# Attention beside a mixture of experts: weighted sums of two attention units in one group, the maxima unit behind the transposition one pair of heads later, and two sets of loads into stacks that are done

## The chip, the cores and the metric

The kernel runs on one core of a Trainium2 chip. The time is that of the device for one launch, in microseconds (us); smaller is better. The engines are TensorE (PE; its weight loads are PEld), VectorE (DVE), ScalarE (ACT), GpSimd (POOL) and SyncE (SP), which issues most of the DMAs. They run side by side and wait for one another by semaphores.

## The reference

The input x has 4 batches of 1024 rows of 256 numbers, in float32. Its rows are normalised (layernorm, xn). The output is x + attention(xn) + experts(xn).

```python
q, k, v = xn @ Wq, xn @ Wk, xn @ Wv                  # 16 heads of 16
scores = where(j <= i, q @ k.T, -1e30) + slope[h] * (j - i)
w = softmax(scores / sqrt(16))
attention = (w @ v) @ Wo + bo
...
# each row goes to the 2 best of 8 experts by router logits
expert(x) = (gelu(x @ Wgate) * (x @ Wup)) @ Wdown * per_expert_scale
experts = sum over the 2 of weight * expert(xn)
```

## The kernel before

The kernel has five stages, one behind the other: `project` (layernorm, the projections, router logits), `route` (the experts' choice), `attend` (attention, and the map of rows to experts on the side), `experts` (72 tiles of 128 rows), `combine`. The change lies in `attend`, and in where the loads of the experts' gate and up weights (`w_gu`) and of the x rows for `combine` go.

`attend` goes through 16 steps t, one for each batch and quad of four heads. The queries and keys of a quad lie as stacks of bf16 parts (`qs`, `ks`, four buffers each, loaded three steps ahead by `load_quad` from SP, L150), so that a single matmul gives scores with float32-like accuracy, with the slope's term and the row's negated maximum as further rows of the stack.

A step has two kinds of work on TensorE.

The first is the scores and sums of this quad. The causal 1024x1024 triangle of a head is cut into 9 attention units of 512 columns (`UNITS`, L55). For each unit and head TensorE makes the scores (`scores`, L831, into the ring `spsum` of three), ScalarE takes their exp into `probs` (`exp`, L778; a unit has one of `PRING` = 3 slots), POOL zeroes the diagonal tiles (`mask_unit`, L715), and TensorE adds the weighted sums of the values for the four heads into `cpsum` (`weighted`, L839). These are float32 matmuls of 17 columns of weights, the four heads in four column tiles of the array (`tile_position`). `weighted` is issued in halves; 8 matmul instructions are 256 columns of all four heads. ScalarE copies `cpsum` to `ctxT` twice a step: the low rows behind the exp of unit 3, head 2 (L798), the high rows behind the first exp of the next step's unit 1 (L802).

The second is the row maxima for a quad one or two steps ahead. They come in maxima units (`ITEMS`, L98; `item` L813 on TensorE, L733 on VectorE): 18 of 1024 columns each into one of two slots of `mpsum` (`RING` = 2), which VectorE reduces (L742), and a nineteenth, number NI - 1 = 18, that transposes the finished maxima (L829); VectorE splits the result into three bf16 parts (L749 to L755), and SP writes it to the stack as further rows (`maxima_rows`, L666). The first score of the next step waits for them.

The order on TensorE is written out by hand. A step has 18 pairs of heads p (`PAIRS`), two for each unit: pairs 0 and 1 score unit 1, 2 and 3 unit 2, and so on, and pairs 16 and 17 score unit 0 of the next step. In a pair come a score, the pair's maxima units (`PAIR_ITEMS`, L107), the other score, and then the weighted sums that `PV_AT` (L92) gives it:

```python
for h in (2 * (p % 2), 2 * (p % 2) + 1):
    scores(n, hq1, u, h)
    if h % 2 == 0:
        for ahead, k in PAIR_ITEMS[p]: item(...)
for u0, half in PV_AT[p]: weighted(t, b, hq, u0, half)
```

Before the change `PV_AT` has groups in pairs 1, 3, 4, 7, 9, 11, 13, 15 and 17: unit 0; unit 1; the low half of unit 2; the high half of unit 2 with unit 3; units 4, 5, 6, 7 and 8. `PAIR_ITEMS` has one maxima unit in each pair: numbers 8 to 17 of the next quad in pairs 0 to 9, and 0 to 7 of the quad after it in pairs 10 to 17, with the transposition ahead of number 1 in pair 11. A maxima unit's matmuls wait until VectorE has taken the one two before. The first exp of a unit waits (L783) until the sums of the unit that had its slot are done.

SP issues, in `attend`, first the lists for POOL's map and the first row of maxima, then the eight loads of `w_gu` (L680), then in each step `load_quad` for three steps ahead, the next quad's row of maxima (L668) and the lists for the map. POOL issues four indirect DMAs per step for the map, behind the masks of unit 2 (L712).

Of the kernel before, what the change touches and what calls it, by code (L numbers as in the profile page):

```python
# [18 lines left out]
P = 128  # L19
F32 = mybir.dt.float32  # L20
# [13 lines left out]
DH = D // P  # L34
# [49 lines left out]


PV = [pv_pieces(u) for u in range(NU)]
PRING = 3
SRING = 3


PAIRS = 2 * NU
PV_AT = [[] for _ in range(PAIRS)]  # L92
for _u in range(NU):
    PV_AT[2 * _u + 1] = [(_u, 0), (_u, 1)]
PV_AT[4], PV_AT[5], PV_AT[7] = [LOW_LAST], [], [HIGH_FIRST, (3, 0), (3, 1)]


ITEMS = []  # L98
# [8 lines left out]
def pair_items():  # L107

    first = NI - 1 - LEAD
    out = [[(1, LEAD + p)] for p in range(first)] + [[(2, k)] for k in range(LEAD)]
    out[first + 1].insert(0, (1, NI - 1))
    return out


# [13 lines left out]
ITEM_NO = item_orders()  # L130


def head_buffers(nc, ctx):

    sb = lambda name, shape, dt=F32: ctx.enter_context(nc.sbuf_tensor(name, shape, dt))
    sem = lambda name: ctx.enter_context(nc.semaphore(name))
    return {
        "qs": [sb(f"qs{i}", [ROWS, 4, S], BF16) for i in range(NQ)],
        "ks": [sb(f"ks{i}", [ROWS, 4, S], BF16) for i in range(NQ)],
        "vs": [sb(f"vs{i}", [P, KT, 4, VW]) for i in range(NQ)],  # L140
        "stack_in": [sem(f"stack_in{i}") for i in range(NQ)],
        "v_in": [sem(f"v_in{i}") for i in range(NQ)],
        "const_in": sem("const_in"),
    }
# [464 lines left out]
def attend(nc, ins, scratch, keep, heads):  # L609
# [3 lines left out]
    with ExitStack() as ctx:  # L613
# [50 lines left out]
        @block.sync  # L664
        def _(sp):
            def maxima_rows(n, hq):  # L666
                sp.wait_ge(max_split, n + 1)
                sp.dma_start(qs[hq][R_MAX:ROWS, :, :], mparts[:, hq % 2, :]).then_inc(mrow_in[hq], 16)  # L668

            def tile_entries(t, par):  # L670

                sp.dma_start(entries[:, par], keep["entries"][:, :, ds(2 * t, 2), :]).then_inc(entries_in[par], 16)
                sp.dma_start(slots[:, par], keep["slot"][:, :, ds(2 * t, 2)]).then_inc(entries_in[par], 16)

            for t in range(2):
                tile_entries(t, t)
            maxima_rows(0, 0)

            for e in range(NE):
                sp.dma_start(keep["w_gu"][:, e * DH:(e + 1) * DH], ins["w_gu"][:, e * DH:(e + 1) * DH]).then_inc(keep["w_gu_in"], 16)  # L680

            def body(t, b, hq, has):
                par = hq % 2
                if has(3):
                    sp.wait_ge(pv_done, PRING + NU * t)
                    load_quad(sp, scratch, heads, *quad(b, hq, 3))
                if has(1):
                    maxima_rows(t + 1, (hq + 1) % NQ)
                sp.wait_ge(entries_out[par], 64 * (2 * b + hq // 2 + 1))
                if has(2):  # L690
                    tile_entries(t + 2, par)

            steps(sp, body)
            for i in range(2):
                sp.wait_ge(entries_out[i], 64 * (B * NQ // 2))

        @block.gpsimd
        def _(pool):
            def body(t, b, hq, has):
                for j in range(1, NU + 1):  # L700
                    if j == NU and not has(1):
                        continue
                    mask_unit(NU * t + j, j % NU)
                    if j == LOW_LAST[0]:
                        map_entries(b, hq)

            def map_entries(b, hq):
                par = hq % 2
                wait_apart(pool, entries_in[par], 32 * (2 * b + hq // 2 + 1))
                for i in range(2):  # L710
                    for k in range(2):
                        pool.indirect_dma_start(scratch["map"], bass.IndirectOffsetOnAxis(ap=slots[:, par, k, i:i + 1].bitcast(U32), axis=0),  # L712
                                                entries[:, par, k, i, :], None).then_inc(entries_out[par], 16)

            def mask_unit(n, u):  # L715

                if not DIAG[u]:
                    return
                wait_apart(pool, exp_done, 4 * n + 4 + SRING)
                for c in DIAG[u]:  # L720
                    part = probs[:, u % PRING, :, c:c + P]
                    pool.affine_select(out=part, in_=part, compare_op=ALU.is_ge, fill=0.0, base=0,  # L722
                                       pattern=[[0, 4], [1, P]], channel_multiplier=-1).then_inc(masked, 1)

            mask_unit(0, 0)
            steps(pool, body)
# [47 lines left out]
        @block.scalar  # L774
        def _(act):
            act.sem_inc(exp_done, SRING)

            def exp(n, u, h):  # L778

                m = 4 * n + h  # L780
                act.wait_ge(s_ready, m + 1)
                if h == 0:
                    act.wait_ge(pv_done, n + 1)  # L783
                act.activation(probs[:, u % PRING, h], spsum[:, (4 * u + h) % SRING], ACT.Exp, scale=SCALE).then_inc(exp_done, 1)  # L784

            for h in range(4):
                exp(0, 0, h)
            exp(1, 1, 0)

            def body(t, b, hq, has):  # L790
                for j in range(1, NU + 1):
                    u, n = j % NU, NU * t + j
                    if j < NU or has(1):
                        for h in range(1 if j == 1 else 0, 4):
                            exp(n, u, h)
                            if (j, h) == (3, 2):
                                act.wait_ge(low_done, t + 1)
                                act.activation(keep["ctxT"][:, ds(t, 1), 0:CH].rearrange("p a c -> p (a c)"), cpsum[:, :], ACT.Copy).then_inc(ctx_taken, 1)  # L798
                if has(1):
                    exp(NU * t + NU + 1, 1, 0)  # L800
                act.wait_ge(pv_done, NU * t + NU + PRING)
                act.activation(keep["ctxT"][:, ds(t, 1), CH:S].rearrange("p a c -> p (a c)"), cpsum[:, :], ACT.Copy).then_inc(ctx_taken, 1)  # L802

            steps(act, body)

        @block.tensor
        def _(pe):
# [31 lines left out]
            def weighted(t, b, hq, u, half):  # L839
# [12 lines left out]
                    pe.wait_ge(masked, MASKED[NU] * t + MASKED[u] + needs)  # L852
                for i, (c, kt, q0, w) in enumerate(pieces):
                    for h in range(4):
                        last = pe.matmul(cpsum[32 * h:32 * h + VW, q0 % CH:q0 % CH + w], vs[hq][:, kt, h], probs[:, u % PRING, h, c:c + w],  # L855
                                         start=i == 0 and (u, half) in ((0, 0), HIGH_FIRST),
                                         stop=(u, half) == LOW_LAST or kt == KT - 1, tile_position=(0, 32 * h), skip_group_check=True)
                if (u, half) == LOW_LAST:
# [16 lines left out]
            def body(t, b, hq, has):  # L875
                for p in range(PAIRS):
                    j = p // 2 + 1
                    u, n = j % NU, NU * t + j
                    b1, hq1 = quad(b, hq, 1) if j == NU else (b, hq)
                    for h in (2 * (p % 2), 2 * (p % 2) + 1):  # L880
                        if j < NU or has(1):
                            if u == 0 and h == 0:
                                pe.wait_ge(mrow_in[hq1], 16 * (b1 + 1))
                            scores(n, hq1, u, h)
                        if h % 2 == 0:
                            for ahead, k in PAIR_ITEMS[p]:
                                if has(ahead):
                                    item(t + ahead, *quad(b, hq, ahead), k)
                    for u0, half in PV_AT[p]:
                        weighted(t, b, hq, u0, half)  # L890

# [363 lines left out]
def build(nc, ins, out):  # L1255
    with ExitStack() as ctx:
# [8 lines left out]
            "slot": sb("slot", [P, 2, NT], I32),  # L1265
            "entries": sb("entries", [P, 2, NT, 2], I32),
            "tile_expert": sb("tile_expert", [1, NST], I32),
            "w_gu": sb("w_gu", [P, NE * DH, 2 * HID]),
            "w_gu_in": ctx.enter_context(nc.semaphore("w_gu_in")),
            "ctxT": sb("ctxT", [P, B * NQ, S]),  # L1270
        }
# [4 lines left out]
            "map": nc.dram_tensor("slot_map", [NST * P, 2], I32).ap(),  # L1276
            "y": nc.dram_tensor("expert_rows", [2 * TOK + NST * P, D], F32).ap(),
        }
        project(nc, ins, scratch, keep)
        with ExitStack() as held:  # L1280
            heads = head_buffers(nc, held)
            route(nc, ins, scratch, keep, heads)
            attend(nc, ins, scratch, keep, heads)
        last_weights = {"w_o": sb("w_o", [P, DH, D]), "bias": sb("bias", [P, D]), "x": sb("x_rows", [P, NT, D]),
                        "in": ctx.enter_context(nc.semaphore("wo_in")), "x_in": ctx.enter_context(nc.semaphore("x_rows_in"))}
        experts(nc, ins, scratch, keep, last_weights)
        combine(nc, ins, scratch, keep, last_weights, out)
# [61 lines left out]
```

## Time and profile before

| | us |
|---|---|
| median of 3 runs | 939.3 |
| lowest, highest | 938.69, 1016.51 |
| the profiled execution | 941.12 |
| its span, first to last instruction | 939.4 |
| mean granted TensorE clock | 0.937 |

| engine | busy us | share |
|---|---|---|
| TensorE matmul | 812.5 | 86% |
| TensorE weight load | 426.3 | 45% |
| VectorE | 562.1 | 60% |
| ScalarE | 483.2 | 51% |
| GpSimd | 390.0 | 42% |

The attention's TensorE work goes from 159.1 to 627.5 us. In a timeline each row is a start in us from the span's start, a length in us, the engine, the line of the kernel, the operation, out<-in with shapes, and how many instructions of that kind the row merges; in brackets stands how long the engine had been idle before it and what ended the wait. TensorE's ends are modelled, so lengths overlap the next start; the time of a piece is the difference of two starts.

### The profile page before, as it was taken

To read this page: it belongs to the slowest core of one execution; us is meant where nothing else is said; L and a number is where in the kernel's file an instruction comes from. 1 tells how busy PE (TensorE), PEld (TensorE's weight loads), DVE (VectorE), ACT (ScalarE), POOL (GpSimd) and SP (SyncE) were. 2 spreads that over 40 slices of the span, in tenths; PEclk is the share of its full clock that TensorE was granted. 3 is DMA by queue.
4 is the path that set the end of the run, shared out by engine and by line. 5 is a ranking of instruction groups with operands and counts; after the bars stand their busy time and mean duration, and the time that the engine had idled before them with its cause. 6 is when DMAs were issued, how large, how long until landed. Compare 5 with 4: busy or idle time off the path is not lost. (4 is left out here: it accounts for less than half of the span.)

```text
span 939.4 us, 17505 instructions
## 1 busy us (share of the span) xinstructions
PE 812.5 (86%) x5618; PEld 426.3 (45%) x5619; DVE 562.1 (60%) x1560; ACT 483.2 (51%) x1011; POOL 390.0 (42%) x456
## 2 busy tenths in 40 slices
PE   5989601799999999999999999856999999999598
PEld 2555400134444444444444444313555656555497
DVE  4767364988888888888888888301222222222177
ACT  2333300067777777777777777852333333333374
POOL 3545340033223233322323332323666666665398
PEclk9999855589999999999999999996999999999799
DMA  4999899295555666555566600009222222222485
GB/s 157 221 263 269 213 107 121 34 253 74 62 61 57 82 81 81 67 62 61 59 82 81 81 3 3 2 6 321 86 84 84 84 84 84 84 85 78 129 245 182
DMA packets 115004, 100.32 MB, mean 107 GB/s; under 512 B 58172, under 2 KB 95676, under 8 KB 114876
## 3 DMA queue, kind: packets, MB, share of 16 engines
q1 hardware_dynamic: 105976, 80.50, 46.9%
q0 software_dynamic: 8960, 18.95, 6.4%
q8 instruction: 37, 0.61, 0.3%
q14 instruction: 31, 0.25, 0.1%
HBM read 63.89 MB, written 35.00 MB: 105 GB/s over the span
## 5 line engine op out<-in xcount | busy, mean ns | idle before, releaser
L784 ACT ACTIVATE probs<-spsum 128x512 f32<-128x512 f32 x576 | 312.1, 604 | 169.6 <-PE spsum L835 163.8
L742 DVE CUSTOM_DVE_ANT_0 junk<-mpsum,mask 128x128 bf16<-128x128 f32 (+7 forms) x512 | 360.0, 754 | 58.5 <-issue 51.7
L824 PE MATMUL mpsum<-ks,qs 102*128 102x512 bf16 (+3 forms) x768 | 183.5, 343 | 45.9 <-DVE cpsum L731 26.3
L722 POOL TENSOR_SCALAR_AFFINE_SELECT probs<-probs 128x512 f32<-128x512 f32 x128 | 78.8, 634 | 340.8 <-ACT probs L784 340.8
L835 PE MATMUL spsum<-qs,ks 105*128 105x512 bf16 (+3 forms) x768 | 199.2, 329 | 10.6 <-ACT probs L784 8.3
L855 PE MATMUL cpsum<-probs,vs 128*17 128x256 f32 (+2 forms) x2560 | 152.7, 360 | 1.5 <-POOL probs L722 0.8
L1037 PE MATMUL gu<-w_gu,xTs 128*128 x288 | 139.2, 607 | 1.7 <-ACT xTs L981 1.7
L1016 DVE COPY hT<-hp 128x256 f32<-128x256 f32 x72 | 30.6, 425 | 167.8 <-PE hp L1044 100.6
L824 PEld LDWEIGHTS mpsum<-ks,qs 102*128 102x128 bf16 x768 | 69.8, 100 | 122.5 <-DVE maxima L742 39.8
L835 PEld LDWEIGHTS spsum<-qs,ks 105*128 105x128 bf16 x768 | 67.1, 97 | 102.9 <-ACT probs L784 52.9
L956 POOL DMA_INDIRECT expert_rows<-y,places x72 | 70.7, 983 | 72.2 <-ACT y L990 42.2
L855 PEld LDWEIGHTS cpsum<-probs,vs 128*17 128x17 f32 x2560 | 59.8, 97 | 77.4 <-issue 36.4
L951 POOL DMA_INDIRECT rows<-xn_rows,places x72 | 69.3, 962 | 34.9 <-issue 20.7
L985 ACT ACTIVATE gate<-gu 128x256 f32<-128x256 f32 x72 | 27.7, 384 | 100.7 <-issue 64.0
L1050 PE MATMUL yp<-w_down,hT 128*128 x288 | 74.2, 380 | 0.4 <-issue 0.4
L1037 PEld LDWEIGHTS gu<-w_gu,xTs 128*128 128x128 f32 x288 | 52.1, 193 | 45.4 <-issue 38.5
L712 POOL DMA_INDIRECT slot_map<-entries_now,slots x64 | 61.8, 966 | 17.2 <-issue 17.2
L417 PE MATMUL qkpsum<-xT,w_qk 128*128 128x512 f32 x128 | 59.8, 612 | 4.4 <-DVE rest L359 3.3
L1014 DVE TENSOR_TENSOR hid<-gu,gate 128x256 f32<-128x256 f32 x72 | 30.2, 420 | 49.3 <-ACT gate L985 49.3
L1050 PEld LDWEIGHTS yp<-w_down,hT 128*128 128x128 f32 x288 | 49.1, 190 | 4.6 <-issue 0.9
L312 POOL TENSOR_TENSOR parts<-rest,parts 128x512 bf16<-128x512 f32 x32 | 37.0, 1157 | 32.0 <-DVE parts L361 32.0
L990 ACT ACTIVATE y<-yp 128x256 f32<-128x256 f32 x72 | 27.7, 384 | 36.2 <-issue 31.8
(124 smaller groups left out, 698.5 us busy)
## 6 DMA issues: line engine op xcount, KB each, us to landing
qk_parts<-parts SPq DMA_DIRECT2D x32, 384.0 KB, 4.4
qs<-qk_parts SPq DMA_DIRECT2D x96, 128.0 KB
ks<-qk_parts SPq DMA_DIRECT2D x96, 128.0 KB
yk<-expert_rows SPq DMA_DIRECT2D x32, 256.0 KB, 3.1
v_rows<-vt SPq DMA_DIRECT2D x32, 136.0 KB, 4.5
vs<-v_rows SPq DMA_DIRECT2D x16, 272.0 KB, 12.0
x_in<-in_x SPq DMA_DIRECT2D x8, 512.0 KB, 6.3
xn_rows<-xn SPq DMA_DIRECT2D x8, 512.0 KB, 5.8
```

The costliest lines, as they stand in the source:

```text
L417: last = pe.matmul(qkpsum[:, q % 2], w_qk[:, dh, q], xT[:, par, dh], start=dh == 0, stop=dh == DH - 1)
L712: pool.indirect_dma_start(scratch["map"], bass.IndirectOffsetOnAxis(ap=slots[:, par, k, i:i + 1].bitcast(U32), axis=0), entries[:, par, k, ...
L722: pool.affine_select(out=part, in_=part, compare_op=ALU.is_ge, fill=0.0, base=0, pattern=[[0, 4], [1, P]], channel_multiplier=-1).then_inc ...
L742: last = dve.tensor_tensor_reduce(junk[:, slot, c:c + w], mpsum[:, slot, c:c + w], keep["mask"][:, S - w:S], 1.0, 3 * NEG, ALU.add, ALU.ma ...
L784: act.activation(probs[:, u % PRING, h], spsum[:, (4 * u + h) % SRING], ACT.Exp, scale=SCALE).then_inc(exp_done, 1)
L824: last = pe.matmul(mpsum[:, slot, at + c:at + e], qs[hq][0:R_MAX, h, qt * P:(qt + 1) * P], ks[hq][0:R_MAX, h, c:e], start=True, stop=True)
L835: last = pe.matmul(spsum[:, (4 * u + h) % SRING, c:c + w], ks[hq][:, h, kt * P:(kt + 1) * P], qs[hq][:, h, q0:q0 + w], start=True, stop=True)
L855: last = pe.matmul(cpsum[32 * h:32 * h + VW, q0 % CH:q0 % CH + w], vs[hq][:, kt, h], probs[:, u % PRING, h, c:c + w], start=i == 0 and (u, ...
L951: pool.indirect_dma_start(rows[:, s % RR], None, scratch["xn"], bass.IndirectOffsetOnAxis(ap=places[:, s, 0:1].bitcast(U32), axis=0)).then ...
L956: pool.indirect_dma_start(scratch["y"], bass.IndirectOffsetOnAxis(ap=places[:, s, 1:2].bitcast(U32), axis=0), y[:, s % RR], None).then_inc ...
L1037: last = pe.matmul(gu[:, par], xT[:, par, dh], w_gu[:, ds(e * DH + dh, 1)].rearrange("p a c -> p (a c)"), start=dh == 0, stop=dh == DH - 1)
L1050: last = pe.matmul(yp[:, par, 0:D], hT[:, par, dh], w_down[:, ds(e * DH + dh, 1)].rearrange("p a c -> p (a c)"), start=dh == 0, stop=dh == ...
```

## The change

- `PRING` goes from 3 to 4, and the slot of a unit in `probs` is its running number n modulo 4 (n = 9 t + u).
- The groups of weighted sums are in pairs 1 (unit 0), 4 (unit 1 and the low half of unit 2), 7 (the high half of unit 2 and unit 3), 11 (units 4 and 5), 15 (6 and 7) and 17 (8).
- The transposition stays in pair 11, alone; maxima unit 1, which stood behind it, goes to pair 12. Where a pair has two units, the second now follows the second score.
- The stacks `qs` and `ks` are one tensor, and `w_gu` (first half of it) and the x rows (second half) are views of the same bytes. The eight loads of `w_gu` go out in steps 13 and 14, four each, when the quads that lay there are done; the x rows are loaded where they were, at the start of `experts`.

```diff
-PRING = 3
+PRING = 4
...
 PAIRS = 2 * NU
 PV_AT = [[] for _ in range(PAIRS)]
-for _u in range(NU):
-    PV_AT[2 * _u + 1] = [(_u, 0), (_u, 1)]
-PV_AT[4], PV_AT[5], PV_AT[7] = [LOW_LAST], [], [HIGH_FIRST, (3, 0), (3, 1)]
+PV_AT[1] = [(0, 0), (0, 1)]
+PV_AT[4] = [(1, 0), (1, 1), LOW_LAST]
+PV_AT[7] = [HIGH_FIRST, (3, 0), (3, 1)]
+PV_AT[11] = [(4, 0), (4, 1), (5, 0), (5, 1)]
+PV_AT[15] = [(6, 0), (6, 1), (7, 0), (7, 1)]
+PV_AT[17] = [(8, 0), (8, 1)]
...
-    out[first + 1].insert(0, (1, NI - 1))
+    out[first + 1], out[first + 2] = [(1, NI - 1)], out[first + 1] + out[first + 2]
...
-def head_buffers(nc, ctx):
+def head_buffers(nc, ctx, stacks):
...
-        "qs": [sb(f"qs{i}", [ROWS, 4, S], BF16) for i in range(NQ)],
-        "ks": [sb(f"ks{i}", [ROWS, 4, S], BF16) for i in range(NQ)],
+        "qs": [stacks[0:ROWS, i, 0] for i in range(NQ)],
+        "ks": [stacks[0:ROWS, i, 1] for i in range(NQ)],
...
-            for e in range(NE):
-                sp.dma_start(keep["w_gu"][:, e * DH:(e + 1) * DH], ins["w_gu"][:, e * DH:(e + 1) * DH]).then_inc(keep["w_gu_in"], 16)
-
             def body(t, b, hq, has):
                 par = hq % 2
                 if has(3):
                     sp.wait_ge(pv_done, PRING + NU * t)
                     load_quad(sp, scratch, heads, *quad(b, hq, 3))
+                elif has(1):
+                    sp.wait_ge(pv_done, PRING + NU * t)
+                    for e in range(NE // 2 * (t % NQ - 1), NE // 2 * (t % NQ)):
+                        sp.dma_start(keep["w_gu"][:, e * DH:(e + 1) * DH], ins["w_gu"][:, e * DH:(e + 1) * DH]).then_inc(keep["w_gu_in"], 16)
...
-                    part = probs[:, u % PRING, :, c:c + P]
+                    part = probs[:, n % PRING, :, c:c + P]
...
-                        if h % 2 == 0:
-                            for ahead, k in PAIR_ITEMS[p]:
-                                if has(ahead):
-                                    item(t + ahead, *quad(b, hq, ahead), k)
+                        for ahead, k in PAIR_ITEMS[p][h % 2:h % 2 + 1]:
+                            if has(ahead):
+                                item(t + ahead, *quad(b, hq, ahead), k)
...
-            "w_gu": sb("w_gu", [P, NE * DH, 2 * HID]),
+            "stacks": sb("stacks", [P, NQ, 2, 4, S], BF16),
...
+        words = lambda a: a.rearrange("p i s h t -> p (i s h t)").bitcast(F32)
+        keep["w_gu"] = words(keep["stacks"][:, 0:2]).rearrange("p (e h) -> p e h", h=2 * HID)
...
-        last_weights = {"w_o": sb("w_o", [P, DH, D]), "bias": sb("bias", [P, D]), "x": sb("x_rows", [P, NT, D]),
+        last_weights = {"w_o": sb("w_o", [P, DH, D]), "bias": sb("bias", [P, D]), "x": words(keep["stacks"][:, 2:4]).rearrange("p (t d) -> p t d", d=D),
```

## Rows read from the trace of the kernel before

**Rows 1.** The page, 40 slices of the span: TensorE's busy share in tenths.
```profile
PE   5989601799999999999999999856999999999598
```

**Rows 2.** Windows: one step, busy us and instructions; then clock, DMA share, GB/s.
```profile
402.54:430.06 27.52, 26.17 (x258) 11.77 (x257) 23.54 (x69) 20.32 (x39) 8.78 (x12) 1.00 0.58 70
```

**Rows 3.** TensorE's timeline, one step and the last step's transposition.
```profile
400.45 1.06 PE L855 MATMUL cpsum<-probs,vs 128*17 128x256 f32 x16
401.44 0.39 PE L835 MATMUL spsum<-qs,ks 105*128 105x512 bf16 x1
401.67 0.60 PE L824 MATMUL mpsum<-ks,qs 102*128 102x512 bf16 x2
402.11 0.59 PE L835 MATMUL spsum<-qs,ks 105*128 105x512 bf16 x2
402.54 0.27 PE L829 MATMUL mpsum<-ident,maxima 128*32 128x128 f32 x1
403.73 0.61 PE L824 MATMUL mpsum<-ks,qs 102*128 102x512 bf16 x3 [0.92 <-DVE maxima L742]
404.18 0.38 PE L835 MATMUL spsum<-qs,ks 105*128 105x512 bf16 x1
404.49 1.06 PE L855 MATMUL cpsum<-probs,vs 128*17 128x256 f32 x16
...
422.75 0.92 PE L835 MATMUL spsum<-qs,ks 105*128 105x512 bf16 x2
...
424.26 1.49 PE L855 MATMUL cpsum<-probs,vs 128*17 128x256 f32 x24
425.68 0.39 PE L835 MATMUL spsum<-qs,ks 105*128 105x512 bf16 x1
...
426.78 0.59 PE L824 MATMUL mpsum<-ks,qs 102*128 102x512 bf16 x2
427.66 0.39 PE L835 MATMUL spsum<-qs,ks 105*128 105x512 bf16 x1 [0.28 <-ACT probs L784]
...
429.19 0.60 PE L824 MATMUL mpsum<-ks,qs 102*128 102x512 bf16 x2
...
595.00 0.27 PE L829 MATMUL mpsum<-ident,maxima 128*32 128x128 f32 x1
595.17 0.39 PE L835 MATMUL spsum<-qs,ks 105*128 105x512 bf16 x1
```

**Rows 4.** VectorE's timeline, in the same step.
```profile
415.00 0.69 DVE L742 CUSTOM_DVE_ANT_0 junk<-mpsum,mask 128x512 bf16<-128x512 f32 x1 [0.31 <-issue]
...
423.36 1.09 DVE L742 CUSTOM_DVE_ANT_0 junk<-mpsum,mask 128x896 bf16<-128x896 f32 x1
...
424.59 0.95 DVE L742 CUSTOM_DVE_ANT_0 junk<-mpsum,mask 128x768 bf16<-128x768 f32 x1
...
427.20 0.82 DVE L742 CUSTOM_DVE_ANT_0 junk<-mpsum,mask 128x640 bf16<-128x640 f32 x1 [1.30 <-issue]
...
429.97 1.23 DVE L742 CUSTOM_DVE_ANT_0 junk<-mpsum,mask 128x1024 bf16<-128x1024 f32 x1 [0.24 <-issue]
...
431.12 0.27 DVE L749 TENSOR_SCALAR mparts<-mpsum 32x128 bf16<-32x128 f32 x1
...
432.60 1.09 DVE L742 CUSTOM_DVE_ANT_0 junk<-mpsum,mask 128x896 bf16<-128x896 f32 x1 [0.33 <-DVE mparts L755]
```

**Rows 5.** ScalarE's timeline, in the same step.
```profile
422.13 0.59 ACT L798 ACTIVATE ctxT<-cpsum 128x512 f32<-128x512 f32 x1
...
427.01 2.07 ACT L784 ACTIVATE probs<-spsum 128x512 f32<-128x512 f32 x4 [1.83 <-PE spsum L835]
```

**Rows 6.** SP's timeline: the weights' loads, and a row of maxima.
```profile
186.71 4.14 SPq L680 DMA_DIRECT2D w_gu<-in_w_gu  x8
...
432.36 0.79 SPq L668 DMA_DIRECT2D qs<-mparts  x1
```

**Rows 7.** POOL's timeline: the fourth indirect DMA of the step.
```profile
424.84 0.96 POOL L712 DMA_INDIRECT slot_map<-entries_now,slots  x1 [0.30 <-issue]
```

More of the change, by code:

```diff
@@ L783, in exp @@
                     act.wait_ge(pv_done, n + 1)
-                act.activation(probs[:, u % PRING, h], spsum[:, (4 * u + h) % SRING], ACT.Exp, scale=SCALE).then_inc(exp_done, 1)
+                act.activation(probs[:, n % PRING, h], spsum[:, (4 * u + h) % SRING], ACT.Exp, scale=SCALE).then_inc(exp_done, 1)
             for h in range(4):
@@ L854, in weighted @@
                     for h in range(4):
-                        last = pe.matmul(cpsum[32 * h:32 * h + VW, q0 % CH:q0 % CH + w], vs[hq][:, kt, h], probs[:, u % PRING, h, c:c + w],
+                        last = pe.matmul(cpsum[32 * h:32 * h + VW, q0 % CH:q0 % CH + w], vs[hq][:, kt, h], probs[:, n % PRING, h, c:c + w],
                                          start=i == 0 and (u, half) in ((0, 0), HIGH_FIRST),
@@ L1278, in build @@
         }
+        words = lambda a: a.rearrange("p i s h t -> p (i s h t)").bitcast(F32)
+        keep["w_gu"] = words(keep["stacks"][:, 0:2]).rearrange("p (e h) -> p e h", h=2 * HID)
         project(nc, ins, scratch, keep)
         with ExitStack() as held:
-            heads = head_buffers(nc, held)
+            heads = head_buffers(nc, held, keep["stacks"])
             route(nc, ins, scratch, keep, heads)
             attend(nc, ins, scratch, keep, heads)
-        last_weights = {"w_o": sb("w_o", [P, DH, D]), "bias": sb("bias", [P, D]), "x": sb("x_rows", [P, NT, D]),
+        last_weights = {"w_o": sb("w_o", [P, DH, D]), "bias": sb("bias", [P, D]), "x": words(keep["stacks"][:, 2:4]).rearrange("p (t d) -> p t d", d=D),
                         "in": ctx.enter_context(nc.semaphore("wo_in")), "x_in": ctx.enter_context(nc.semaphore("x_rows_in"))}
```

## The prediction

> **What bounds the kernel now.** I read the page's slices first: TensorE is busy for nine tenths or more of each slice of the attention, a little less where it begins and ends [rows 1]. The change touches attention and two sets of loads, so everything is decided there. The windows view of one step (one batch's quad of four heads, transposition to transposition) gives 27.52 us: TensorE 26.17 busy at a granted clock of 1.00, the upper level throughout, VectorE 23.54, ScalarE 20.32 [rows 2]. No engine is far from the limit, so I turned to TensorE's own order of time, where the starts matter, not the busy time, because its ends are modelled.
>
> There the pieces are (starts subtracted, [rows 3]):
> - A maxima unit of 1024 columns is 2 matmuls: 401.67 to 402.11, 0.44 us. A score matmul of 512 columns is 0.22 (two of them from 402.11 to 402.54). A pair of heads, with two scores and a unit, is 0.87.
> - A group of 16 weighted-sum matmuls (one attention unit) lasts from 400.45 to 401.44, 0.99; one of 24 at this width from 424.26 to 425.68, 1.42. Eight more cost 0.43, so 16 are 0.86 of work, and 0.13 goes when TensorE leaves the column tiles. Entering costs too: the score at 404.18 is followed by the group 0.31 later, where a score is otherwise 0.22. A group in and out costs 0.22.
> - The transposition at 402.54 is followed by a maxima unit only at 403.73: 1.19, of which the row puts 0.92 down to VectorE. In the last step no maxima unit stands behind it and it takes 0.17 (595.00 to 595.17). The stall is 1.02.
> - From 426.78 to 427.66 a maxima unit takes 0.88, not 0.44: 0.44 of wait for ScalarE. Two scores at 422.75 last 0.92, where two last 0.59 at 402.11: 0.33 more.
> The stalls of a step are 1.02 + 0.44 + 0.33 = 1.79; what is left, 25.73, is issue.
>
> VectorE is the other half. A maxima unit of two tiles takes 1.23 from start to start (423.36 to 424.59), one of a single 1024-column tile 1.15 (429.97 to 431.12) [rows 4]. A step has 14 of the former and 4 of the latter, 21.8, and the transposition's four instructions with what follows, 431.12 to 432.60, 1.48: 23.3 us. The other 4.2 are gaps of 0.2 to 0.4 after a single group and one of 1.30 after the long group at 424.26 [rows 4]. They come from the ring of two mpsum slots: while TensorE is in a group, VectorE has at most two units left, 2.4 us less what it had done of them.
>
> **The change, part by part.**
> *Fewer groups.* Nine groups per step become six (pairs 1, 4, 7, 11, 15, 17): 3 x 0.22 = 0.66 us less issue, 10.6 us over 16 steps. The matmuls are the same.
> The TensorEngine Tiling (Array Packing) page of the Trainium skill (Key Properties) says that a change of tiling mode drains the array, and its page TensorE: Matmul & The Clock Gate (Step-by-step: what each phase is for) puts a drain at some 128 cycles. By that an estimate for entry and exit at the upper clock would be 0.11 us, half of what the rows show, and 5 us in place of 10.6; I go by the rows.
>
> *Unit behind the transposition later.* The transposition stays in pair 11; the unit behind it follows the first score of pair 12. Between them come a score (0.22), a double group (4 x 0.43 + 0.22 = 1.94) and a score: 2.4 us, more than the stall. The 1.02 goes. But pair 12 now has two units.
>
> *Four probability slots.* The exp of unit 5 must wait today for the first sum of the group at 424.26; after that wait ScalarE resumes at 427.01, although its score began at 425.68 and 0.43 is the usual distance, and this gives TensorE's 0.44 [rows 3, 5]. With four slots it waits for unit 1, summed in pair 4, long before. No other unit's slot is late either: unit 6 needs unit 2 (pair 7), 7 needs 3 (pair 7), 8 needs 4 (pair 11), and so on. The 0.44 goes. The 0.33 stays: a copy of the sums sits in ScalarE's order at 422.13 [rows 5].
>
> *What is late next.* Bunching leaves stretches in which TensorE makes a maxima unit every 0.87 us and VectorE takes one every 1.22, with two slots between. Set TensorE's leaving of a group at 0. Score to 0.22, unit to 0.66, its last matmul at 0.44; VectorE, idle by then, begins 0.55 behind that, at 1.0 (the unit at 429.19 has its second matmul 0.22 later, at 429.41, and VectorE, which had idled for 0.24, starts on it at 429.97: 0.55 [rows 3, 4]) and is through at 2.3 (1.23 and the 0.08 of the last read), so the third unit behind a group can't start before 2.35, the fourth before 3.6, then one per 1.23.
> - Pairs 12 to 15 hold 8 scores and 5 units, 3.95 of issue. The fifth starts at 4.8, and with it and a score the stretch ends at 5.5: 1.55 of stall (before, with groups in pairs 13 and 15: none).
> - Pairs 2 to 4: the third unit could start at 1.96: 0.40.
> - Pairs 5 to 7: the same wait, most of it within the 0.33 of ScalarE: 0.35 in all.
> - Pairs 8 to 11: 0.40 for the unit of pair 10, and 0.35 for the transposition, which waits for the unit of pair 9.
> Sum 3.05 against 1.79 before: +1.26. VectorE tells the same: its gaps become about 0.9 + 1.4 + 0.3 + 0.5 + 0.8 + 0.8 = 4.7 (a gap grows by what a group grows, 0.86 to 0.93 over the 0.3 to 0.5 of a single one), and 23.3 + 4.7 = 28.0.
> This is worked from starts and not shown by any row, so bounds: no new stall at all (-0.66 - 1.02 - 0.44 = -2.1 us a step), if VectorE's gap behind a double group were the 0.3 of a single one; and +2.6, if after every long group the signals come late as at 427.01 (below).
>
> *Gate and up weights.* Eight loads are issued from 186.71 on, ahead of a quad's loads [rows 6]. They now go out four and four in steps 13 and 14, where SP has no quad to load. Behind them on SP is the row of maxima, which goes out 2.3 us after the transposition (432.36 against 430.06), two thirds of a step, some 17 us, behind the loads; eight of these took 4.14 us to issue, so four are long out of the way. The experts use them only after the attention. Cost 0, with the 17 us as cover; without it a row of maxima would come late by up to the 4.14 that eight take to issue, in steps 13 and 14: 0 to 8 us. The x rows go to another address at the same moment: 0.
>
> *Sum.* A full step: -0.66 + 1.26 = +0.6. Fourteen of them 8.4; step 14 lacks the units for two steps ahead, step 15 has none and ScalarE sets its pace: +0.7 together. +9 us. The profiled execution took 941.1 (span 939.4), so 950.2; the runs shown have 939.3 as median, 1.8 below it: 948. Chances below go by 2%, 19 us, which is about what a measurement of this kernel can tell from no change.
>
> **Rivals.**
> *Signals late after each long group (slower).* Behind the group of 24 (1.42 us) ScalarE begins 1.33 after the score's start instead of 0.43, and VectorE at 427.20, 0.5 late as well [rows 3 to 5]. If the length of the group does that, and not unit 5's wait nor POOL's fourth indirect DMA at 424.84, which ends beside it [rows 7], the change has four such groups (1.42, 1.42, 1.94, 1.94). Each puts 0.5 into VectorE's round, which now sets the pace, and 0.9 in front of ScalarE, so between 0.5 and 0.9, say 0.67, for each of three more: +2.0 a step on top of 0.6. 16 x 2.6 = 41: 980. It turns to slower by over 2% from two more late groups on (+1.3 a step): 962. Against it: unit 5's wait explains ScalarE's part, and behind the group of 16 at 400.45 nothing is late.
> *VectorE keeps up (faster).* Issue and stalls removed, nothing new: -2.1 x 15 = -32, 907. It needs VectorE's gaps at 25.4 - 23.3 = 2.1 over six groups, 0.35 each; rows show that behind single groups, but 1.30 behind the long one. Half of it gives 923.
> *Everything cancels.* The stalls of pairs 12 to 15 come out a third smaller, and the time stays at 939 to 941. The same mechanism with other sizes; it lies in the forecast's range.
>
> **How the numbers follow.** Forecast with its sizes (935 to 960): 0.63. Late signals: 0.22, of which 0.19 beyond 958. VectorE keeps up, wholly or half: 0.15, of which 0.10 beyond -19 us. The range 924 to 972 leaves out the full late signals (about 0.11) and the full gain (0.08). Likeliest 948, its own range 935 to 960. Faster 0.10, same 0.70, slower 0.20.
>
> **What would show it.** Right: steps of 27.9 to 28.3; groups of 32 matmuls 1.85 long; no 0.92 behind the transposition; new waits of TensorE for VectorE in pairs 12 to 15, three of them, adding to about 1.5; the exp of unit 5 no more than 0.45 behind its score. Wrong: a step below 27, with VectorE's gap behind the double groups under 0.6 (then VectorE isn't what sets the pace), or gaps of 1.3 to 1.9 behind every long group (the late signals). TensorE's waits for a row of maxima in steps 14 and 15 would show the weights' loads in the way.

## The result, and the profile after

The kernel after the change takes 959.8 us as median against 940.4 of the kernel before beside it: a ratio of 1.020, with an interval of 1.016 to 1.023. One of the four runs of the kernel before, of 1016.5 us, fell in a slower state of the chip and is left out of the ratio; the median of its other three is 939.3. So it is slower, by 19 to 20 us, where 9 were forecast; whether that is over 2% the interval leaves open. The profiled execution was its quickest run, 955.5 us, with a span of 953.8 against 939.4.

The 14.4 us between the spans come from two places. From the first maxima matmul to the last weighted sum the attention takes 485.7 us against 468.2, +17.4. The experts take 236.0 against 238.7, -2.7, and that is no part of the change: two of the experiments below, `ring4` and `later`, have the same code there and take 238.6 and 235.9. What differs is the granted clock of the first 10 us of that stage, 0.50 before and 0.77 after.

The attention is read from one step, as in [rows 2]. First the page's slices of the kernel after, to be set beside [rows 1]:

```profile
PE   5999502799999999999999999983999999999598
```

The windows view of the ninth step after (columns as in [rows 2]):

```profile
409.60:438.22 28.62, 26.29 (x258) 11.97 (x258) 23.28 (x69) 20.26 (x39) 8.81 (x12) 1.00 0.57 67
```

The step is 1.1 us longer than in [rows 2] at the same clock, with the same count of instructions and VectorE's and ScalarE's busy time hardly changed. The busy columns say nothing of the cause; the starts do. TensorE's timeline of the same step after:

```profile
409.61 0.27 PE L833 MATMUL mpsum<-ident,maxima 128*32 128x128 f32 x1 [0.20 <-DVE maxima L746]
409.71 0.38 PE L839 MATMUL spsum<-stacks 105*128 105x512 bf16 x1
410.02 1.92 PE L859 MATMUL cpsum<-probs,vs 128*17 128x256 f32 x32
411.88 0.39 PE L839 MATMUL spsum<-stacks 105*128 105x512 bf16 x1
...
413.19 0.38 PE L839 MATMUL spsum<-stacks 105*128 105x512 bf16 x1
414.25 0.61 PE L828 MATMUL mpsum<-stacks 102*128 102x512 bf16 x3 [0.67 <-DVE maxima L746]
...
415.47 0.61 PE L828 MATMUL mpsum<-stacks 102*128 102x512 bf16 x2 [0.18 <-DVE maxima L746]
...
416.69 0.61 PE L828 MATMUL mpsum<-stacks 102*128 102x512 bf16 x3 [0.18 <-DVE maxima L746]
...
427.35 0.61 PE L828 MATMUL mpsum<-stacks 102*128 102x512 bf16 x3 [0.23 <-DVE maxima L746]
...
429.54 0.39 PE L839 MATMUL spsum<-stacks 105*128 105x512 bf16 x1
...
431.17 0.39 PE L839 MATMUL spsum<-stacks 105*128 105x512 bf16 x1
432.14 0.39 PE L839 MATMUL spsum<-stacks 105*128 105x512 bf16 x1 [0.58 <-ACT probs L788]
...
434.54 0.39 PE L839 MATMUL spsum<-stacks 105*128 105x512 bf16 x1
...
437.00 0.59 PE L828 MATMUL mpsum<-stacks 102*128 102x512 bf16 x2 [0.28 <-DVE maxima L746]
...
438.22 0.27 PE L833 MATMUL mpsum<-ident,maxima 128*32 128x128 f32 x1 [0.20 <-DVE maxima L746]
```

Read it against [rows 3]. The transposition is followed by a score after 0.10, so the 1.02 behind it is gone. The groups of 32 last 1.86 (410.02 to 411.88), as forecast. The prices are again differences of starts less 0.22 for a matmul of 512 columns (the row's own figure in brackets is smaller, since it goes by modelled ends):

| stretch | stalls in the row order | sum | forecast |
|---|---|---|---|
| pairs 12 to 15 | 0.83, 0.34, 0.34 | 1.51 | 1.55 |
| pairs 2 to 4 | 0.39 | 0.39 | 0.40 |
| pairs 5 to 7 | 0.10, 0.76 | 0.86 | 0.35 |
| pairs 8 to 11 | 0.45, 0.36 | 0.81 | 0.75 |
| all | | 3.57 | 3.05 |

What is left, 28.62 - 3.57 = 25.05, is issue, 0.64 less than the 27.52 - 1.83 = 25.69 of the step before: 0.21 for each of three groups saved, as the rows had it (0.22). The 1.83 is taken from starts too: 0.44, 0.31 for the copy, and 1.08 behind the transposition, which takes 0.11 where nothing holds it (409.61 to 409.71); the prediction's 1.02 had 0.17 for it, from the last step. The estimate from the Trainium skill's page TensorE: Matmul & The Clock Gate (Step-by-step: what each phase is for), 0.11 for a way in and out, is not what this kernel shows.

So one line is off, pairs 5 to 7. There stands ScalarE, whose timeline after (the first of the two) answers to [rows 5], and beside it POOL's (the second), which answers to [rows 7]:

```profile
430.51 0.60 ACT L788 ACTIVATE probs<-spsum 128x512 f32<-128x512 f32 x1 [1.70 <-PE spsum L839]
...
435.18 4.23 ACT L788 ACTIVATE probs<-spsum 128x512 f32<-128x512 f32 x8 [1.10 <-PE spsum L839]
```

```profile
429.19 0.98 POOL L716 DMA_INDIRECT slot_map<-entries_now,slots  x1 [0.16 <-issue]
430.47 0.96 POOL L716 DMA_INDIRECT slot_map<-entries_now,slots  x1 [0.31 <-issue]
431.74 0.96 POOL L716 DMA_INDIRECT slot_map<-entries_now,slots  x1 [0.30 <-issue]
433.00 0.96 POOL L716 DMA_INDIRECT slot_map<-entries_now,slots  x1 [0.30 <-issue]
```

The exp begins 0.97 behind the start of its score (429.54 to 430.51), where 0.43 is usual, and that of unit 5 0.64 behind (434.54 to 435.18), although its slot is long free. They begin 1.32 and 5.99 behind the start of POOL's first indirect DMA at 429.19. The second distance is the one of the kernel before. POOL's first of the four there:

```profile
421.04 0.98 POOL L712 DMA_INDIRECT slot_map<-entries_now,slots  x1 [0.16 <-issue]
```

The exp of unit 5 at 427.01 [rows 5] stands 5.97 behind 421.04, and in all full steps of both kernels the distance of unit 5's exp lies between 5.92 and 6.05. That is a mark of POOL's DMAs, not of a slot that comes free. The experiments test it.

### The profile page after: what moved, and what is told of

The parts are those of the page before. It is cut to its first block and busy times, and to the rows that moved or that the text cites. A ratio compares the mean times of both kernels' runs of the same rounds, so it can differ in the third digit from the quotient of the medians.

```text
span 953.8 us, 17505 instructions
## 1 busy us (share of the span) xinstructions
PE 817.6 (86%) x5618; PEld 429.6 (45%) x5619; DVE 558.2 (59%) x1560; ACT 482.2 (51%) x1011; POOL 390.9 (41%) x456
## 5 line engine op out<-in xcount | busy, mean ns | idle before, releaser
L746 DVE CUSTOM_DVE_ANT_0 junk<-mpsum,mask 128x128 bf16<-128x128 f32 (+7 forms) x512 | 356.4, 754 | 77.1 <-issue 59.2
L828 PE MATMUL mpsum<-stacks 102*128 102x512 bf16 (+3 forms) x768 | 184.0, 344 | 53.5 <-DVE cpsum L735 26.4
L839 PE MATMUL spsum<-stacks 105*128 105x512 bf16 (+3 forms) x768 | 197.6, 330 | 11.1 <-ACT probs L788 7.1
L859 PE MATMUL cpsum<-probs,vs 128*17 128x256 f32 (+2 forms) x2560 | 145.0, 363 | 0.4 <-ACT ctxT L806 0.2
L1040 PE MATMUL gu<-stacks,xTs 128*128 x288 | 137.3, 599 | 1.8 <-ACT xTs L984 1.8
L828 PEld LDWEIGHTS mpsum<-stacks 102*128 102x128 bf16 x768 | 67.1, 100 | 140.2 <-DVE maxima L746 54.1
L839 PEld LDWEIGHTS spsum<-stacks 105*128 105x128 bf16 x768 | 68.4, 97 | 97.4 <-ACT probs L788 34.5
L859 PEld LDWEIGHTS cpsum<-probs,vs 128*17 128x17 f32 x2560 | 64.8, 98 | 71.4 <-issue 29.7
L1040 PEld LDWEIGHTS gu<-stacks,xTs 128*128 128x128 f32 x288 | 51.6, 191 | 44.5 <-issue 37.6
```

Source lines behind the costliest of these rows:

```text
L746: last = dve.tensor_tensor_reduce(junk[:, slot, c:c + w], mpsum[:, slot, c:c + w], keep["mask"][:, S - w:S], 1.0, 3 * NEG, ALU.add, ALU.ma ...
L828: last = pe.matmul(mpsum[:, slot, at + c:at + e], qs[hq][0:R_MAX, h, qt * P:(qt + 1) * P], ks[hq][0:R_MAX, h, c:e], start=True, stop=True)
L839: last = pe.matmul(spsum[:, (4 * u + h) % SRING, c:c + w], ks[hq][:, h, kt * P:(kt + 1) * P], qs[hq][:, h, q0:q0 + w], start=True, stop=True)
L1040: last = pe.matmul(gu[:, par], xT[:, par, dh], w_gu[:, ds(e * DH + dh, 1)].rearrange("p a c -> p (a c)"), start=dh == 0, stop=dh == DH - 1)
```

## The experiments

Changes are described against the kernel after, save `before_spread`, which changes the kernel before. "Step" is the mean distance of two transpositions over 14 steps, "last step" what lies between the last transposition and the last weighted sum.

| kernel | ratio to before | step us | last step us |
|---|---|---|---|
| before | 1 | 27.49 | 32.22 |
| after | 1.020 (1.016 to 1.023) | 28.53 | 35.11 |
| ring4 | 0.9996 (0.998 to 1.001) | 27.39 | 32.11 |
| later | 0.9975 (0.996 to 0.999) | 27.27 | 32.09 |
| groups | 1.022 (1.020 to 1.024) | 28.77 | 34.91 |
| map8 | 1.059 (1.056 to 1.063) | 30.63 | 33.85 |
| after_mapend | 1 run | 28.08 | 32.27 |
| later_mapend | 1 run | 26.93 | 31.11 |
| after_half | 1 run | 26.67 | 34.88 |
| before_spread | 0.9939 (0.992 to 0.996) | 27.05 | 31.60 |
| after_spread | 1.012 (1.010 to 1.015) | 28.37 | 32.50 |
| later_spread | 0.9939 (0.992 to 0.996) | 26.93 | 31.59 |
| placed | 0.987 (0.984 to 0.989) | 26.58 | 31.27 |

**One part at a time: ring4, later, groups.** `ring4` puts back the groups and the places of the maxima units, and so keeps the fourth slot and the loads into the stacks:

```diff
-PV_AT[1] = [(0, 0), (0, 1)]
...
-PV_AT[17] = [(8, 0), (8, 1)]
+for _u in range(NU):
+    PV_AT[2 * _u + 1] = [(_u, 0), (_u, 1)]
+PV_AT[4], PV_AT[5], PV_AT[7] = [LOW_LAST], [], [HIGH_FIRST, (3, 0), (3, 1)]
...
-    out[first + 1], out[first + 2] = [(1, NI - 1)], out[first + 1] + out[first + 2]
+    out[first + 1].insert(0, (1, NI - 1))
```

`later` puts back the groups alone, `groups` the places alone.

> The changed kernel with the old groups of weighted sums and the old place of the maxima unit behind the transposition; what is left of the change is the fourth probability slot and the two sets of loads. Theory 1 (the slot: ScalarE resumes late at unit 5 because it waits for the slot): the exp of unit 5 begins 0.43 us behind its score, a step falls from 27.5 to 27.1 us, the time by some 6 us to 934. Theory 2 (POOL's four indirect DMAs hold up the waking of engines that wait): the exp of unit 5 still begins 5.9 to 6.0 us after the first of the step's four indirect DMAs, a step stays at 27.4 to 27.5 and the time at 939 to 941. The loads cost nothing by either.

> As ring4 but with the maxima unit behind the transposition in pair 12, as in the change; old groups. The 1.08 us stall behind the transposition goes from pair 11; by the ring of two mpsum slots most of it comes back as one wait of about 0.9 in pairs 12 and 13, so a step is 0.2 us shorter than in ring4: 27.3, the time 3 us under ring4's. The rival (the stall was a pure loss that cover removes) gives 1.0 less: 26.5 and 15 us under ring4's.

> As ring4 but with the new six groups of weighted sums; the unit behind the transposition stays in pair 11. If the groups are what costs, with three of them 0.66 us less issue and the waits for VectorE in pairs 12 to 15, 8 to 11 and 2 to 4 more, a step is 0.2 above the changed kernel's 28.55: 28.7 to 28.9, the time 962 to 965. If it is the combination of both edits that costs (two units in pair 12), a step is at or below 27.5 and the time at or below 941.

`ring4`: 937.6 us against 937.8. The slots and the loads together are worth nothing measurable. With four slots the exp of unit 5 still begins 1.21 behind its score (422.79 to 424.00), which is 5.86 behind POOL's first indirect DMA, and TensorE still waits 0.33 for it. ScalarE's timeline, then POOL's:

```profile
424.00 2.06 ACT L785 ACTIVATE probs<-spsum 128x512 f32<-128x512 f32 x4 [1.72 <-PE spsum L836]
```

```profile
418.14 0.98 POOL L713 DMA_INDIRECT slot_map<-entries_now,slots  x1 [0.16 <-issue]
```

`later`: 936.0 us. The 1.02 behind the transposition goes, but the step is only 0.12 shorter than in `ring4`. TensorE's timeline shows the wait again, one pair later, for the same VectorE:

```profile
400.82 0.27 PE L830 MATMUL mpsum<-ident,maxima 128*32 128x128 f32 x1
400.93 0.38 PE L836 MATMUL spsum<-stacks 105*128 105x512 bf16 x1
...
403.55 0.38 PE L836 MATMUL spsum<-stacks 105*128 105x512 bf16 x1
404.72 0.61 PE L825 MATMUL mpsum<-stacks 102*128 102x512 bf16 x3 [0.80 <-DVE maxima L743]
```

`groups`: 958.8 us, +21, all of the loss and a little more. So the six groups carry it. Its mean step of 28.77 holds one of 30.20, in which TensorE's clock fell for 3.4 us; without that one it is 28.66, so moving the unit takes 0.13 a step off with the new groups, as it takes 0.12 off with the old ones. The windows row of the fall:

```profile
354.72:358.13 3.41, 3.41 (x31) 1.25 (x33) 1.83 (x7) 0.60 (x1) 0.00 (x0) 0.50 0.08 8
```

**POOL's indirect DMAs elsewhere: map8.** The four are issued behind the masks of unit 8, near the end of the step's row of units, where the groups around them have 24 and 16 matmuls.

```diff
-                    if j == LOW_LAST[0]:
+                    if j == 8:
                         map_entries(b, hq)
```

> The changed kernel with POOL's four indirect DMAs of a step issued behind the masks of unit 8 (pair 15 on) instead of unit 2 (pair 4 on). Theory 2 (they hold up waking engines): the waits of pairs 5 to 8 beyond the ring's own (some 0.4 to 0.5 us a step) go, and late wakings now stand within 6 us of the new place, where TensorE waits for no one: step 28.0 to 28.15, the time 6 to 8 us under the changed kernel's. Theory 1 or a cause in the long groups themselves: the late wakings stay behind the groups of pairs 4 and 7 and a step stays at 28.5.

It takes 992.7 us, 5.9% more than before, and a step 30.63 where 28.0 to 28.15 were expected. The lateness went with the DMAs (the exp of unit 5 now begins 0.43 behind its score), but it grew, and TensorE does wait at the new place. Four timelines of `map8` show it: POOL's, TensorE's, ScalarE's and VectorE's, in this order.

```profile
402.93 0.98 POOL L716 DMA_INDIRECT slot_map<-entries_now,slots  x1 [0.16 <-issue]
...
406.75 0.96 POOL L716 DMA_INDIRECT slot_map<-entries_now,slots  x1 [0.30 <-issue]
```

```profile
405.38 0.39 PE L839 MATMUL spsum<-stacks 105*128 105x384 bf16 x2
...
406.48 0.60 PE L828 MATMUL mpsum<-stacks 102*128 102x512 bf16 x2
409.23 0.39 PE L839 MATMUL spsum<-stacks 105*128 105x384 bf16 x2 [2.16 <-ACT probs L788]
```

```profile
408.58 0.60 ACT L788 ACTIVATE probs<-spsum 128x512 f32<-128x512 f32 x1 [3.39 <-remote]
```

```profile
408.76 0.69 DVE L746 CUSTOM_DVE_ANT_0 junk<-mpsum,mask 128x512 bf16<-128x512 f32 x1 [2.69 <-issue]
```

The score starts at 405.38 and its exp at 408.58, 3.20 behind it instead of 0.43; VectorE, whose maxima unit starts at 405.60, waits as well and begins 0.18 behind ScalarE. Two engines that wait for different semaphores start together, 5.65 and 5.83 behind POOL's first indirect DMA. The group ahead of it is one of 24, no longer than one of the kernel before; neither its length nor a slot explains 2.8 us.

The trace's semaphore events, which no view prints, say what is late. TensorE's scores of 405.38, 406.04 and 406.26 have their signals to ScalarE at 408.56, 408.64 and 408.69, its maxima units of 405.60 and 406.48 theirs to VectorE at 408.60 and 408.73: five signals of 1.1 us of work within 0.17 us, the first of them 2.8 late. It is the same in the other runs: in the full steps of the seven kernels with four DMAs in a row, and of `after_spread` below, 129 exps that ScalarE was free for begin late, and each of them begins 0.02 behind the recorded signal of a score, the distance of the punctual ones; what is longer is the way from the score's start to that signal, 0.5 to 3.5 us instead of 0.40. So "late wakings" here are late signals of TensorE, as far as these events tell, and this is why two engines are late together. Some events are missing while the DMAs go out (527 of the 576 signals of scores are recorded in the kernel before, all of them with the DMAs behind the attention), so they don't tell how a signal is held.

**The DMAs taken out of the attention: after_mapend, later_mapend.** POOL issues all 64 behind the attention, and SP no longer waits for them in each step (the gap between attention and experts grows from 13 to 95 us, so only steps are compared, not times).

```diff
-                    if j == LOW_LAST[0]:
-                        map_entries(b, hq)
...
             steps(pool, body)
+            for g in range(NT):
+                for k in range(2):
+                    pool.indirect_dma_start(scratch["map"], ...)
```

> The changed kernel with all 64 indirect DMAs of the map issued by POOL behind the last step, so none beside the attention; the total grows by their 64 x 1.27 us, 81 us, and only the attention's steps are read. Theory 2 (the indirect DMAs hold up waking engines, up to about 6 us from a step's first): a step falls from 28.55 to 28.1, which is issue plus the waits of the ring; no exp begins more than 0.1 behind its ready score save behind a copy of the sums. Rival (the late wakings belong to the long groups): 28.5 as before.

> The same for the kernel with the old nine groups, four slots and the unit behind the transposition in pair 12. Theory 2: a step falls from 27.27 to 26.95 (the 0.30 at unit 5). The difference to after_mapend, 1.1 to 1.2, is then the price of the six groups by the ring of two alone: 0.65 less issue, 1.8 more waits. Rival: 27.27 and a difference of 1.3.

Steps of 28.08 and 26.93, and no exp late within a full step. Windows and TensorE's stretch of pairs 5 to 7 in `after_mapend`, with one stall of 0.31 (427.35 to 428.11) where there were 0.10 and 0.76:

```profile
405.88:433.97 28.09, 26.15 (x258) 11.98 (x259) 23.20 (x69) 20.33 (x39) 4.93 (x8) 1.00 0.57 68
```

```profile
426.91 0.60 PE L830 MATMUL mpsum<-stacks 102*128 102x512 bf16 x3
427.35 0.92 PE L841 MATMUL spsum<-stacks 105*128 105x512 bf16 x2
428.11 0.61 PE L830 MATMUL mpsum<-stacks 102*128 102x512 bf16 x3
```

Its stalls are 1.51, 0.39, 0.31 and 0.85, together 3.06, where the forecast had worked out 3.05. The waits for the ring of two slots are what the prediction said; and with late wakings gone from both, six groups instead of nine cost 28.08 - 26.93 = 1.15 us a step: 1.8 more of waits, 0.65 less of issue. POOL's masks are still in these steps, and nothing is late.

**One DMA at a time: before_spread, after_spread, later_spread.** The four go out one each behind the masks of units 1, 2, 7 and 8; nothing else changes. `before_spread` does this to the kernel before.

```diff
+MAP_AT = [1, 2, 7, 8]
...
-                    if j == LOW_LAST[0]:
-                        map_entries(b, hq)
+                    if j in MAP_AT:
+                        map_entries(b, hq, MAP_AT.index(j))
```

> The kernel before, three slots and nine groups, with the same four DMAs issued one each behind the masks of units 1, 2, 7 and 8. If the wait of 0.44 us at unit 5 was a waking held up by the DMAs and not the wait for its probability slot: step 27.05 to 27.1 (27.49 before), 0.992 to 0.994 of before. If it was the slot: step 27.5, 1.000. If both: the 0.44 stays here and went only with both changed.

> The whole change, with POOL's four indirect DMAs of a step issued one each behind the masks of units 1, 2, 7 and 8 instead of four in a row behind unit 2. If the change's loss is the ring's waits of the six groups plus wakings held up by the four DMAs in a row: step 28.1 us (as with the DMAs behind the attention) instead of 28.53, the last step's end some 2.5 shorter, together 0.45 x 14 + 2.5 = 9 us, so 1.009 to 1.011 of before. If the late wakings belong to long groups whatever POOL does: 1.018 to 1.022, step 28.5.

> Old nine groups, four slots, unit behind the transposition in pair 12, and the four indirect DMAs of a step one each behind the masks of units 1, 2, 7 and 8 instead of all four behind unit 2. If each holds up wakings for about a microsecond and a half and four in a row add up, single ones are mostly hidden in the rings: step 27.0 (27.27 less the 0.30 at unit 5), the time 4 us under later's, 0.7% under the kernel before. If each one costs its hold by itself wherever it stands, a step gets up to 1 us longer: 28.2 and 950.

`before_spread` is the cleanest test: still three slots, still nine groups, and the step falls from 27.49 to 27.05, the 0.44 exactly. In TensorE's timeline the place that had 0.88 in [rows 3] has 0.44 (423.90 to 424.34), and ScalarE follows the score of 422.81 after 0.42:

```profile
422.81 0.39 PE L837 MATMUL spsum<-qs,ks 105*128 105x512 bf16 x1
...
423.90 0.59 PE L826 MATMUL mpsum<-ks,qs 102*128 102x512 bf16 x2
424.34 0.38 PE L837 MATMUL spsum<-qs,ks 105*128 105x512 bf16 x1
```

```profile
423.23 2.23 ACT L786 ACTIVATE probs<-spsum 128x512 f32<-128x512 f32 x4 [0.93 <-PE spsum L837]
```

`after_spread` came out at 1.012, just above what was expected (1.009 to 1.011): in five of the 14 steps the end of the group of pair 4 still falls on one indirect DMA, and they take 28.6. The other nine take 28.2, because VectorE begins 0.15 late behind the same DMA. One is enough to hold an engine. POOL's and ScalarE's timelines:

```profile
427.23 0.98 POOL L718 DMA_INDIRECT slot_map<-entries_now,slots  x1 [0.17 <-issue]
```

```profile
428.56 0.60 ACT L790 ACTIVATE probs<-spsum 128x512 f32<-128x512 f32 x1 [1.71 <-PE spsum L841]
```

Its exp begins 1.33 behind the DMA, as the one at 430.51 in the kernel after does (1.32), and 0.99 behind its score at 427.57. `later_spread` takes 26.93, the step of `later_mapend`: with nine groups, single DMAs at these places cost nothing.

**VectorE's load halved: after_half.** Each maximum is taken over the second half of its columns alone; the other half of the reduction is left out, and the scale of the exp is made smaller by 1024 so that no value overflows.

```diff
-last = dve.tensor_tensor_reduce(junk[:, slot, c:c + w], mpsum[:, slot, c:c + w], keep["mask"][:, S - w:S], ...
+v = w // 2
+last = dve.tensor_tensor_reduce(junk[:, slot, c + v:c + w], mpsum[:, slot, c + v:c + w], keep["mask"][:, 0:v], ...
```

> The changed kernel with VectorE reducing only half of the columns of each maxima tile (so part of the maxima is left out, and the exp has a smaller scale so that it stays finite). VectorE's unit falls from 1.23 to about 0.7 us, under TensorE's 0.87 for a pair. If the ring of two mpsum slots and VectorE's pace cause the waits of pairs 12 to 15, 2 to 4 and 8 to 11, they go: step 28.55 - 1.5 - 0.4 - 0.7 = 25.5 to 26.0. If something in the long groups themselves costs, a step stays above 27.5.

The step falls to 26.67, below the 26.93 of nine groups with a full VectorE. That is less than was expected, because the late wakings stay (0.54 and 0.27 of the 1.67 of stalls that are left in one step). Its windows row, VectorE's busy time at 14.48:

```profile
389.10:415.74 26.64, 25.93 (x259) 12.11 (x257) 14.48 (x69) 19.79 (x39) 8.80 (x12) 1.00 0.60 72
```

So most of what six groups cost comes through VectorE: of the 1.51 in pairs 12 to 15 it leaves 0.30, and of the 0.39 in pairs 2 to 4 nothing. VectorE stands still while a long group runs and can't catch up behind it with two slots ahead of it. Nine groups with VectorE's load halved were not run, so what six would gain over nine there is not shown.

**A better order: placed.** Nine groups, four slots, the DMAs spread, and the maxima units placed by halves of a pair so that they stand apart:

```diff
+ITEM_AT = [0, 1, 4, 6, 9, 10, 12, 14, 17, 17, 20, 23, 24, 25, 28, 29, 31, 32, 35]
...
+    for x, item in zip(ITEM_AT, seq):
+        out[x // 2][x % 2].append(item)
```

> Nine groups, four slots, DMAs spread, unit behind the transposition later, and the maxima units placed by half pairs so that behind each group the first unit follows the first score and the others stand further apart. If waits of TensorE for the ring are what is left beside issue (25.0 + 1.27 in the kernel without the placing, 26.95 with what the stalls list leaves out), the placing takes 0.2 to 0.4 us a step: step 26.6 to 26.75, 0.988 to 0.990 of before. If VectorE's 23.3 and its gaps set the pace in any order: step 26.95, 0.993 to 0.995.

928.7 us against 940.2: 1.3% faster than before and, by the two ratios (0.987 / 1.020), 3.2% faster than after. The step is 26.58, below what was expected, and two stalls are left in it, 0.60 for VectorE and 0.31 behind a copy of the sums. The first, in TensorE's timeline:

```profile
403.04 0.60 PE L840 MATMUL spsum<-stacks 105*128 105x384 bf16 x4
404.09 0.61 PE L829 MATMUL mpsum<-stacks 102*128 102x512 bf16 x3 [0.44 <-DVE maxima L747]
```

## Why the prediction was right in part, and where it failed

- *Fewer groups*, -0.66 a step: right. 25.05 of issue against 25.69 is -0.64.
- *Unit behind the transposition later*: right that the 1.02 goes from its place. As a gain it was cancelled already without the new groups: `later` is only 0.12 a step shorter than `ring4`, because the wait comes back one pair later.
- *What is late next*: right, place by place. 1.51 for 1.55, 0.39 for 0.40, 0.31 for 0.35 and 0.85 for 0.75 where wakings are undisturbed; the full step of `after_mapend` is 28.08, the forecast 27.52 + 0.6 = 28.1.
- *Four probability slots* is the step that failed: "The 0.44 goes." The trace of before put the wait beside two things, the slot wait of unit 5 and POOL's fourth indirect DMA, and I took the slot because the program has such a wait there. `ring4` (slot free, wait still there) and `before_spread` (slot unchanged, wait gone) show that it was the DMAs alone. So 0.44 a step was booked as a gain that never came: in the kernel after, late signals cost 28.53 - 28.08 = 0.45 a step, 6.3 us over 14 steps. Without this step the sum would have been near 15 us.
- *Steps 14 and 15*, +0.7 together, was too little: the last step is 2.9 us longer. Its exp of unit 5 is held as before (TensorE waits 1.40), and then the clock falls, which no step of the prediction had. TensorE's timeline of the kernel after, then its windows row for the long group:

```profile
632.54 2.35 PE L839 MATMUL spsum<-stacks 105*128 105x512 bf16 x5 [1.40 <-ACT probs L788]
634.82 3.61 PE L859 MATMUL cpsum<-probs,vs 128*17 128x256 f32 x32
638.36 0.82 PE L839 MATMUL spsum<-stacks 105*128 105x512 bf16 x3
```

```profile
634.82:638.36 3.54, 3.54 (x34) 1.25 (x33) 0.00 (x0) 1.09 (x3) 0.00 (x0) 0.52 0.00 0
```

  The group takes 3.54 at a granted clock of 0.52, close to the lower level of 1.2 GHz, where 1.85 is usual at 2.4: 1.69 us. With the 1.14 that the wait of 1.40 has over the 0.26 of `after_mapend`, that makes up the difference between 35.11 and the 32.27 of `after_mapend`. Ahead of the wait's end TensorE was busy for 5.78 of 8.13 us. That doesn't explain the fall: in the kernel before it was busy for 5.33 of the 8.13 us up to the same place, had waited 1.42, and the clock stayed at 1.00. Its row there:

```profile
616.84 0.39 PE L835 MATMUL spsum<-qs,ks 105*128 105x512 bf16 x1 [1.42 <-ACT probs L784]
```

  Why the clock falls in one and not in the other stays open.
- *Gate and up weights*, 0: right. SP's timeline after; the row of maxima of that step goes out at 583.21, 16 us behind the first four loads:

```profile
565.25 1.78 SPq L690 DMA_DIRECT2D stacks<-in_w_gu  x4
```

- The sum: in the profiled execution the attention grew by 14 x 1.04 + 2.9 = 17.5 us (17.4 between its ends), where 9 were forecast: 6.3 from the slot step, and some 2 from the last steps. The medians lie 19.3 to 20.5 apart; the profiled execution of the kernel after was its quickest.
- The rival *Signals late after each long group* named the right effect and the wrong condition. `map8` has its lateness of 2.8 behind a group of 24, `after_mapend` has none behind groups of 32. What it assumed of the signals themselves, that they come late, is what the semaphore events show. The prediction named POOL's DMA only as what might speak against this rival, and gave it neither a price nor a chance of its own. *VectorE keeps up* is refuted by the ring's waits; `after_half` shows what it would take.

Of the whole, the timed runs on one chip say: spreading the DMAs is worth 0.6% to the kernel before, and with them spread in both, the change costs 951.5 / 934.9 = 1.8%. What stays open is how a signal is held, and by what rule: why a run of four lets some go 1.3 behind the first and others only at 5.7 to 6.0.

## What to carry to other kernels

A queue of two slots between a producer and an engine that is busy for 23.3 of 27.5 us is paid for by even spacing; grouping the producer's other work saves a switch of 0.22 and opens a gap of 0.9 that the slower engine can't make up. When a wait of the trace has two possible causes beside it, don't book its removal on the strength of the one that the program text suggests: look in all steps for what the late starts keep a fixed distance to, which here POOL's timeline shows. And small DMAs that one engine issues in a row can cost the others time: place them apart, and look at who waits for a signal while they are issued.

## What the runs showed of the hardware that was not expected

- While POOL issues indirect DMAs (0.96 us each, one per 1.27), TensorE's signals to ScalarE and VectorE may come late, several at once, and both engines start late with them: by 0.2 to 1.2 us with four in a row behind unit 2, by 2.8 behind unit 8 in the step shown, by 0.15 to 0.6 with a single one. Masks on POOL (1.23 for two) held nobody in `after_mapend`. What in the issue does this was not tested.
- In the last step, with a wait of 1.40 us for ScalarE, TensorE's clock fell to 0.52 for 3.5 us in the kernel after, and to 0.50 in `groups` and `after_half`, which wait 1.27 and 1.30 there; these are the three with groups of 32 and such a wait. It stayed at 1.00 in the kernel before, `ring4` and `later`, with waits of 1.42, 1.31 and 1.29 in the same place and nine groups, and in all kernels whose wait there was 0.26. In `groups` it fell once more, to 0.50 for 3.4 us in a full step, behind waits of 0.20 and 0.79 at the transposition that the step at 412.21 has too, without a fall. Why it falls was not tested.
